# Attention scores in three passes of the rounded 32-bit form instead of one 32-bit product

## The reference

```python
q = x @ wq.T                      # 16 heads of 64
kv = x @ wkv.T                    # one key and one value head
q = _rmsnorm(_rope(q), q_norm_w)
k = _rmsnorm(_rope(k), k_norm_w)
scores = jnp.einsum('bqgtd,bqgsd->bqgts', q, k) * scale
scores = jnp.where(mask[None, None, None], scores, NEG)
attn = jax.nn.softmax(scores, axis=-1)
out = jnp.einsum('bqgts,bqgsd->bqgtd', attn, v)
```

## Time and profile before

| | |
|---|---|
| median of 3 runs | 2087.33 us (2084.66 to 2089.99) |
| the profiled execution | 2087.74 us, span of its instructions 2085.9 us |
| TensorE busy | 1932.8 us, 93% of the span |
| TensorE weight loads busy | 1381.4 us, 66% |
| VectorE busy | 1498.7 us, 72% |
| ScalarE busy | 1386.3 us, 66% |
| GpSimd busy | 904.0 us, 43% |
| score products L1137, 1024 records | 264.0 us busy, 380 ns each |
| mean granted TensorE clock | 0.971 of full speed |

### The profile page before, as it was taken

How to read it: one execution, slowest core, us unless ns; L and a number is a source line. 1 busy time by engine, 2 the same in 40 slices (tenths; PEclk the granted TensorE clock), 3 DMA queues, 4 the chain that set the end, 5 groups by cost and what they waited for, 6 DMA issues and landing times. The chain is left out here.

```text
span 2085.9 us, 33189 instructions
## 1 busy us (share of the span) xinstructions
PE 1932.8 (93%) x9637; PEld 1381.4 (66%) x9637; DVE 1498.7 (72%) x3307; ACT 1386.3 (66%) x3864; POOL 904.0 (43%) x1544
## 2 busy tenths in 40 slices
PE   4999999999999879999669999999999999959998
PEld 2777777777777668777456666666666666635554
DVE  5777878787878655666567888887888787745554
ACT  1567767677777534444358888888888888835554
POOL 0122222222222100322468888888888878641100
PEclk9999999999999889999779999999999999979999
DMA  3211111111111000000000000000000000000000
GB/s 116 79 39 40 38 38 39 38 39 37 41 36 34 1 0 1 1 1 1 1 1 2 1 1 2 1 1 1 1 2 1 1 1 1 2 1 8 11 11 13
DMA packets 28094, 35.60 MB, mean 17 GB/s; under 512 B 13740, under 2 KB 14380, under 8 KB 27660
## 3 DMA queue, kind: packets, MB, share of 16 engines
q1 hardware_dynamic: 27916, 33.49, 5.7%
HBM read 12.09 MB, written 2.10 MB: 7 GB/s over the span
## 5 line engine op out<-in xcount | busy, mean ns | idle before, releaser
L1379 ACT ACTIVATE apb<-ps,amx 128x128 f32<-128x128 f32 x1024 | 361.9, 368 | 63.7 <-DVE amx L1251 62.4
L1494 POOL TENSOR_TENSOR apb<-apb,arc 128x512 f32<-128x512 f32 x256 | 266.4, 1041 | 72.0 <-DVE arc L1259 70.1
L1251 DVE TENSOR_REDUCE amx<-ps 128x4 f32<-128x512 f32 x256 | 175.8, 687 | 155.4 <-PE ps L1137 155.4
L1137 PE MATMUL ps<-akT,aqT 128*128 128x256 f32 x1024 | 264.0, 380 | 0.0
L564 POOL TENSOR_TENSOR h0h<-h0h,const 128x1 fp32r<-128x1 f32 x256 | 46.1, 217 | 400.8 <-DVE h0l L464 400.8
L1137 PEld LDWEIGHTS ps<-akT,aqT 128*128 128x128 f32 x1024 | 197.3, 193 | 21.3
L1379 ACT ACTIVATION_READ_ACCUMULATOR apb<-ps,amx 128x1 f32 x1024 | 211.1, 206 | 0.0
L464 DVE SCALAR_TENSOR_TENSOR h0l<-ps,h0h 128x1024 fp32r<-128x1024 f32 x128 | 156.0, 1219 | 68.6 <-ACT h0h L382 68.6
L65 PE MATMUL ps<-h0h,w123h 128*128 128x512 f32 x512 | 204.1, 399 | 0.0
L66 PE MATMUL ps<-h0l,w123h 128*128 128x512 f32 x512 | 203.3, 397 | 0.0
L67 PE MATMUL ps<-h0h,w123l 128*128 128x512 f32 x512 | 203.2, 397 | 0.0
(11 more groups left out here) (300 smaller groups left out, 5045.4 us busy)
## 6 DMA issues: line engine op xcount, KB each, us to landing
x0k<-x0h SPq DMA_DIRECT2D x128, 72.0 KB
x<-in_x SPq DMA_DIRECT2D x32, 192.0 KB, 2.6
x0k<-x0l SPq DMA_DIRECT2D x64, 72.0 KB
x0k<-x0h SPq DMA_DIRECT2D x64, 48.0 KB
out<-fyo SPq DMA_DIRECT2D x16, 128.0 KB, 2.0
x0k<-x0l SPq DMA_DIRECT2D x32, 48.0 KB
h<-in_w SPq DMA_DIRECT2D x1, 1024.0 KB, 7.7
mw<-in_mw SPq DMA_DIRECT2D x1, 1024.0 KB, 5.0
```

The lines of the kernel that those rows point to most:

```text
L1137: last = pe.matmul(bank[:, p * 2 * T:(p + 1) * 2 * T], qT[:, i % 2, 2 * k + p, :], kT[:, i // 4 % 2, i % 4, :, :].rearrange("p a s -> p (a ...
L1251: ve.tensor_reduce(mx[:, n % 4, :], ps[:, SB[n % 2], :].rearrange("p (h s) -> p h s", h=4), AX_X, ALU.max, negate=True).then_inc(S["mx"], 1)
L1379: last = ac.activation(pb[:, i % 2, head, :], ps[:, SB[n % 2], h * T:(h + 1) * T], ACT.Exp, bias=mx[:, k, h:h + 1], accum_out=sm[:, i % 2, ...
L1494: po.tensor_tensor(p, p, rc[:, i % 2, 4 * k:4 * k + 4].unsqueeze(2).to_broadcast([T, 4, T]), ALU.mult).then_inc(S["pn"], 1)
```

## The change

Keys and queries are no longer kept as plain 32-bit numbers but as a high part in the rounded form and a low part, and the scores become three products of the rounded form. ScalarE's two copies write the high parts, with the same instructions in the same places. VectorE gets two new steps: `low_q` in each even slot behind the sum of squares, which subtracts the high part from the transposed queries in PSUM, and `low_k` in slot 14, two subtractions on 64 partitions each. The transposes that reuse the two banks, and the scores, wait for the new semaphores `ql` and `kl`. The query parts are put into the memory of the convolutions' weights, and the low keys are cleared once like the high ones.

```diff
-        kT = sb("akT", [2 * DH, 2, 4, 2, T])
+        kTh, kTl = (sb(n, [2 * DH, 2, 4, 2, T], F32R) for n in ("akTh", "akTl"))
...
-        qT = sb("aqT", [2 * DH, 2, HH, T])
+        qTh, qTl = (V[n][:].rearrange("p (b h) t -> p b h t", b=2) for n in ("w123h", "w123l"))
...
-                    readers.append(("kT", q + 1))
+                    readers.append(("kl", q + 1))
...
                     if m >= 1:
-                        pe.wait_ge(S["qT"], m)
+                        pe.wait_ge(S["ql"], m)
...
                     if n % 16 == 0:
-                        pe.wait_ge(S["kT"], i // 4 + 1)
-                    pe.wait_ge(S["qT"], 2 * i + k // 2 + 1)
+                        pe.wait_ge(S["kl"], i // 4 + 1)
+                    pe.wait_ge(S["ql"], 2 * i + k // 2 + 1)
...
                     for p in range(2):
-                        last = pe.matmul(bank[:, p * 2 * T:(p + 1) * 2 * T], qT[:, i % 2, 2 * k + p, :],
-                                         kT[:, i // 4 % 2, i % 4, :, :].rearrange("p a s -> p (a s)"), start=False,
-                                         stop=True, skip_group_check=True)
+                        to = bank[:, p * 2 * T:(p + 1) * 2 * T]
+                        qh, ql = qTh[:, i % 2, 2 * k + p, :], qTl[:, i % 2, 2 * k + p, :]
+                        kh, kl = (t[:, i // 4 % 2, i % 4, :, :].rearrange("p a s -> p (a s)") for t in (kTh, kTl))
+                        pe.matmul(to, qh, kh, start=False, stop=False, skip_group_check=True)
+                        pe.matmul(to, qh, kl, start=False, stop=False, skip_group_check=True)
+                        last = pe.matmul(to, ql, kh, start=False, stop=True, skip_group_check=True)
...
+                def low_q(m):
+                    i, h = m // 2, m % 2
+                    ve.wait_ge(S["qT"], m + 1)
+                    ve.tensor_tensor(qTl[:, i % 2, 4 * h:4 * h + 4, :], ps[:, QT, :].rearrange("p (h t) -> p h t", h=4),
+                                     qTh[:, i % 2, 4 * h:4 * h + 4, :].bitcast(F32), ALU.subtract).then_inc(S["ql"], 1)
+
+                def low_k(q):
+                    ve.wait_ge(S["kT"], q + 1)
+                    for a in range(2):
+                        rows = slice(a * DH, (a + 1) * DH)
+                        last = ve.tensor_tensor(kTl[rows, q % 2, :, a, :], ps[rows, XB, :].rearrange("p (r s) -> p r s", r=4),
+                                                kTh[rows, q % 2, :, a, :].bitcast(F32), ALU.subtract)
+                    last.then_inc(S["kl"], 1)
...
-                ve.memset(kT[:], 0.0).then_inc(S["set"], 1)
+                ve.memset(kTh[:].bitcast(F32), 0.0)
+                ve.memset(kTl[:].bitcast(F32), 0.0).then_inc(S["set"], 1)
...
                     if u - 1 in at_q:
                         sum_q(at_q[u - 1])
+                    if u - 1 in at_qt:
+                        low_q(at_qt[u - 1])
+                    if u - 1 in at_kt:
+                        low_k(at_kt[u - 1])
```

More of the change, by code:

```diff
@@ L1061, in attention_phase @@
         names = ("set", "xp", "xn", "xt", "xa", "kv", "kp", "vs", "ka", "ks", "kss", "kln", "rk", "km", "kn", "kt", "kT",
-                 "q", "rope", "sq", "qr", "ssq", "lrq", "rq", "qm", "qt", "qT", "s", "mx", "ex", "rc", "pn", "pt", "pT",
+                 "q", "rope", "sq", "qr", "ssq", "lrq", "rq", "qm", "qt", "qT", "ql", "kl", "s", "mx", "ex", "rc", "pn", "pt", "pT",
                  "pv", "oT", "wo", "y", "tr", "yt", "res", "st", "mv", "all")
@@ L1340, in keep_k @@
                         rows = slice(a * DH, (a + 1) * DH)
-                        last = ac.activation(kT[rows, q % 2, :, a, :],
+                        last = ac.activation(kTh[rows, q % 2, :, a, :],
                                              ps[rows, XB, :].rearrange("p (r s) -> p r s", r=4), ACT.Copy)
@@ L1367, in keep_q @@
                         ac.wait_ge(S["s"], 4 * (i - 2) + 2 * h + 2)
-                    ac.activation(qT[:, i % 2, 4 * h:4 * h + 4, :], ps[:, QT, :].rearrange("p (h t) -> p h t", h=4),
+                    ac.activation(qTh[:, i % 2, 4 * h:4 * h + 4, :], ps[:, QT, :].rearrange("p (h t) -> p h t", h=4),
                                   ACT.Copy).then_inc(S["qT"], 1)
```

## The result

The changed kernel takes 2103.85 us (median of 4 executions, 2100.49 to 2104.38) against 2086.69 us before (2084.66 to 2089.99): a ratio of 1.0077, 95% interval 1.006 to 1.0095. The forecast was 2104. The profiled execution is the fastest of the four, 2100.49 us with a span of 2098.7 us, so the traces differ by 12.8 us and the medians by 17.2.

What follows compares the result with a forecast made beforehand. TensorE was taken to set the pace nearly everywhere, with VectorE and a GpSimd chain close behind. Group terms +1.43, -0.33, +0.46, -0.56 make +1.0 us, sixteen groups 16 us, with clearing 16.5: 2104 us, range 2080 to 2130.

Steps and rivals of the forecast that it cites:

- four parts: 16-slot group cut at VectorE's maxima of slots 0, 2, 6, 10 and next 0: -0.33, +0.46, -0.56, +1.43 us.
- Scores: TensorE, each slot: six rounded records at 0.121 us replace four 32-bit ones of 0.86 us in all, giving back 0.14 us.
- Low parts of the queries: VectorE, even slots: one subtraction behind the sum of squares, 0.60 us of queue each, 4.8 us a group.
- Low parts of the keys: VectorE, slot 14: two subtractions on 64 partitions, 1.2 us, or 0.6 us if 64 partitions cost half.
- Chain: From VectorE's rotation over GpSimd to TensorE's query transpose and scores; ends slots 0 to 2 (6.02 us), 2 to 6 (11.89).
- Waits: Query transposes and scores waiting for low parts: costed at nothing, some 0.1 us a group if the cover is gone.
- Clearing: Second clearing of 128x2048 on VectorE before the attention phase, 1.76 us, about two thirds hidden: 0.5 us.
- The sum: Attention phase: +1.0 us a group, sixteen groups 16 us, with the clearing 16.5 us; 2104 us, chance 0.60.
- Hiding: Rival: low parts vanish in idle time, TensorE's gain arrives in part, -14 us, 2073 us; chance 0.12.
- half: Rival: a lead of about 0.5 us removes most of the loss, +0.2 us a group, 2091 us; chance 0.13.
- VectorE outright: Rival: VectorE is the bound, all 6.0 us a group appear, +96 us, 2184 us; chance 0.03.
- The clock: Rival: longer stalls lower TensorE's clock, its attention work grows some 37 us at mean 0.95, 2120 to 2140 us; chance 0.07.

Runs made afterwards that it cites:

- e5: Changed kernel with GpSimd's scaling of the queries put ahead of its scaling of the probabilities in even slots: 2073.59 us, ratio 0.9936.
- e6: Kernel before the change with GpSimd's scaling of the queries put ahead of its scaling of the probabilities: 2062.00 us, ratio 0.988.
- e11: Changed kernel with the query low parts of slots 4, 6 and 8 cut to four columns: 2103.07 us, ratio 1.0077.
- e12: Changed kernel with the query low parts of slots 10, 12 and 14 cut to four columns: 2089.82 us, ratio 1.0008.
- e1: Changed kernel without VectorE's low-part subtractions, the three rounded passes kept (scores come out doubled): 2065.01 us, ratio 0.9892.

## Why the prediction was right, point by point

**What bounds the kernel.** That TensorE is the bound only in places, with VectorE and the GpSimd chain close behind, is what e5, e6 and e11 show: a shorter chain makes both kernels faster, and less work for VectorE in slots 4, 6 and 8 makes the changed one no faster. The cut into four parts held.

**Scores.** Six records at 0.12 us each, as the row of the last convolution said: from mask to transposes 0.94 us (1300.74 to 1301.68), against 1.09 before.

```profile
1300.74 0.39 PE L1134 MATMUL ps<-maskb,identb 128*128 128x512 bf16 x1
...
1301.21 0.28 PE L1142 MATMUL ps<-akTh,w123l 128*128 128x256 f32 x1
1301.32 0.28 PE L1140 MATMUL ps<-akTh,w123h 128*128 128x256 f32 x1
...
1301.68 0.27 PE L1151 MATMUL ps<-const,apb 128*128 128x128 f32 x1
```

In the TensorE-bound part it is 0.16 us a slot, not 0.14 (13.39 against 14.05 over four slots). The estimate of three quarters of the old time, made from the four passes that "FP8 and Floating Point Precision" (TensorE Precision Notes) of the Trainium skill counts, would have been 0.21; the trace lies between and nearer to the row.

**Low parts of the queries.** 0.60 us each in the queue (1307.72 to 1308.32), and paid only where forecast: nothing in slots 4, 6 and 8 by experiment (e11), 0.50 us for 0.50 us in slots 12 and 14 (e12), and 0.58 us in slot 2 (part 2 to 6 is 11.32 us in e1 and 11.90 here, and slot 4 has no share in that). In slot 10 the forecast's own idle time covers it, and slot 0's lies beside the chain (part 0 to 2 is 6.03 us with and without it).

**Low parts of the keys.** This step was mis-sized. I took 1.2 us, and it is 1.54 with what it does to the maximum behind it. In part 10 to 0 this was offset by a second term, the idle time that the additions could use: 1.57 us by the sum, 1.80 in truth. A bracket counts from the end of a record, but an instruction of this kind lasts 0.67 to 0.69 us and the next can start after 0.60, so each of the three gaps was some 0.08 us wider than its bracket. 16.67 - 1.80 + 1.80 + 1.54 is 18.21, and 18.19 was measured. That 18.10 came so close is luck in part: two errors of 0.34 and 0.23 us against each other.

**Chain.** Parts 0 to 2 and 2 to 6 came out within 0.01 us, and e5 shows that shortening the chain shortens them. The stalls were forecast too long: 2.3 us in slot 5 and about 1 us in slots 1 and 13, measured 1.75, 0.67 and 0.63, and slot 15's 0.49 was not forecast. In slot 5, 0.22 us of the difference is the wait for VectorE's copy two slots earlier, which makes TensorE arrive later; the rest I have not traced. The end of a part is set by the chain, and so did not move.

**Waits.** They were costed at nothing, and in the changed kernel nothing is what they cost. In slots 13 and 15, where TensorE stalls, the low part of the half before has ended 0.83 us before the query transpose starts (1352.04 and 1352.87, 1357.91 and 1358.74). The shortest such distance in a group is 0.63 us, in slots 3 and 11, where the forecast had at least 0.8, and TensorE does not stall there. One line of the waits from 1100 to 1840 us seems to say otherwise:

```profile
PEld ps L1122 <- DVE w123l L1275: 26.8, 28, 1.0
```

It is idle time of the weight loads, two a group, in slots 13 and 15; the transposes that belong to them carry GpSimd's scaling in their brackets. Scores 0 come within 0.1 us of the low keys (1359.21 and the mask at 1359.31), as forecast. In e5, with the chain short, TensorE does stand idle for 0.69 us there (low keys until 1349.88, mask at 1349.98), but VectorE's queue sets the end of that part.

**Clearing.** From the first clearing to the first transposes 5.97 us (1038.69 to 1044.66) against 5.27 before (1040.01 to 1045.28): 0.7 us, forecast 0.5. The transposes now wait for VectorE's low weights, and before for GpSimd's input.

**The sum.** Sixteen groups at +1.0 was wrong at the end. In the trace the first group adds 1.0, the next fourteen 14.5, but the last group up to its last maximum is 1.7 us shorter (38.7 against 40.4): no queries are prepared in its later slots, so it is TensorE-bound and only gains (in e1, without low parts, it takes 38.7 us too). I had named this and let it cancel against the first group, which it does not. The attention phase of the profiled executions, from clearing to last maximum, is 14.1 us longer (807.55 against 793.42), not 16.5, and the stretch before it was 1.3 us shorter in that execution. That the medians differ by 17.2, and so meet the 16.5, is partly the spread of single executions (4 to 5 us), so that the forecast of 2104 met the median within 0.2 us is luck to that extent. The interval of the ratio allows a loss of 12.5 to 19.8 us and holds both numbers.

**Rivals.** Hiding and half: no lead removed the loss, parts 2 to 6 and 10 to 0 grew as forecast. VectorE outright: e11 says no. "Perfetto Trace Analysis" (Identifying the Most-Contended Engine) of the Trainium skill would have TensorE's headroom judged not by matmul busy time but by its weight loads and its share of the peak arithmetic rate, and the weight loads spoke for that rival; the runs bear it out only for slots 2, 12 and 14 and for the keys' step, where VectorE's added time arrived in full. The clock stayed at 1.00 in the group's stretch, with TensorE at 45.36 of 49.51 us. At a mean of 0.95 it would have cost about 40 us (753 / 0.95 - 753), not 37 as the prediction has it. The rounded form gave what it should.

## What to carry to other kernels

Where engines take turns as the bound within a repeating pattern, cut the pattern at the places where the bound changes, and price a change in each part by itself: VectorE's 0.6 us was worth nothing in slots 4, 6, 8 and 10 and about its full time in slots 2, 12 and 14, and TensorE's gain too arrived only in part. When idle time between brackets is to be filled, count it from start to start, for the brackets understate it. A step taken off the bound does not bring its time if a chain through a third engine is next, so look for the order of work on that engine: moving one GpSimd step ahead of another was worth 25 us in the kernel before and 30 in the changed one, more than the whole change. Before splitting operands to save passes, ask whether the engine that makes the low parts has idle time in the same slots.

## What the runs showed of the hardware that was not expected

Two subtractions on 64 partitions in a row occupied VectorE's queue for 0.69 and 0.72 us, and the 128-partition maximum behind them for 0.73, though the same kinds on 128 partitions start 0.59 to 0.60 us apart. In each of the three cases the next instruction starts 0.01 to 0.03 us after the end of the record before it (in the group of the result 1358.52, 1359.24 and 1359.96), where otherwise it starts some 0.08 us before that end. By the kernel's text each of the three reads a memory whose last reader on VectorE began at another partition (0 or 64). That this is the cause was not tried. Six rounded products with six weight loads of 0.19 us each run at 0.12 us a product: in the slot shown above, neighbouring loads start 0.12 us apart, so they overlap.
